# Last tile of a decoder kernel: where the output norm's power, the weights' splits and the norms of expert 0's base rows stand

## The reference

```python
x = x + attn(layernorm(x), ...)                  # blockwise attention
x = x + xattn(layernorm(x), ctx, ...)            # 16 heads, output normed with ln_scale, ln_bias
x = x + ffn(layernorm(x), Wr, br, W1, b1, W2, b2)

def ffn(inputs, Wr, br, W1, b1, W2, b2):         # N = 4096 rows, E = 8, C = 512
    probs = softmax(x @ Wr + br)
    gate, idx = max(probs), argmax(probs)
    pos = cumsum(one_hot(idx)) * one_hot(idx)    # place in the expert; kept where pos < C
    h = relu(expert_in @ W1 + b1)                # expert_in: rows gathered by (idx, pos), times gate
    eo = h @ W2 + b2
    out = gate * eo, put back to the rows
```

## Time and profile before

| what | us |
|---|---|
| median of 3 runs | 1316.72 |
| lowest and highest of them | 1315.18, 1317.61 |
| span of the profiled execution | 1317.2 |

### The profile page before, as it was taken

One profiled execution on the slowest core, in us unless ns is written; L12 is line 12 of the kernel. 1 busy time (PEld: TensorE's weight loads), 2 busy tenths in 40 slices (PEclk: granted clock), 3 DMA queues, 4 the chain that ended last, 5 costly groups with the idle time before them and its releaser, 6 DMA issues.

```text
span 1317.2 us, 31656 instructions
## 1 busy us (share of the span) xinstructions
PE 1286.3 (98%) x12357; PEld 1042.3 (79%) x12357; DVE 937.1 (71%) x1879; ACT 668.0 (51%) x1868; POOL 413.6 (31%) x477
## 2 busy tenths in 40 slices
PE   8999999999999999999999999999999999999998
PEld 7978667777777788888888888888888886888886
DVE  6539778888776676777767777777776786665563
ACT  4447434333333655655556555565555663654552
POOL 3213445454442012213131222312211223455453
PEclk9999999999999999999999999999999999999999
DMA  8962142232323201103021021120202103665530
GB/s 263 325 227 65 58 154 81 84 98 75 107 87 124 81 9 41 49 17 105 17 73 50 18 87 36 41 81 9 73 25 89 65 10 129 228 195 177 177 104 22
DMA packets 69233, 123.75 MB, mean 94 GB/s; under 512 B 12313, under 2 KB 20529, under 8 KB 69090
## 3 DMA queue, kind: packets, MB, share of 16 engines
q1 hardware_dynamic: 60770, 98.17, 22.4%
q0 software_dynamic: 8320, 23.62, 5.1%
HBM read 83.19 MB, written 42.07 MB: 95 GB/s over the span
## 4 chain that ended last, share of the span: by engine, by line
PE 80%; DVE 9%; ACT 4%; DMA 4%; issue 2%; SPq 1%; POOL 0%; DVEq 0%; POOLq 0%; ACTq 0%
PE bank L71 18%; PE bank L73 16%; PE bank L72 16%; PE bank L2335 6%; PE bank L2323 6%; PE bank L2356 4%; PE bank L2348 2%; PE bank L1269 2%; PE bank L1299 2%; DMA raw<-in_L_xattn_Wkv_dram 1%; ACT b_prob L1640 1%; PE bank L1243 1%; DMA raw<-in_L_attn_Wqkv_dram 1%; PE bank L2407 1%; PE bank L2888 1%
## 5 line engine op out<-in xcount | busy, mean ns | idle before, releaser
L1640 ACT ACTIVATE b_prob<-bank,b_neg_top 128x155 f32<-128x155 f32 x496 | 187.3, 407 | 115.6 <-DVE b_neg_top L1852 106.1
L71 PE MATMUL bank<-turned_h,big_h 128*128 128x512 f32 x320 | 130.8, 409 | 1.1 <-DVE turned_l L2106 0.8
L73 PE MATMUL bank<-turned_h,big_l 128*128 128x512 f32 x320 | 125.3, 392 | 0.0
L72 PE MATMUL bank<-turned_l,big_h 128*128 128x512 f32 x320 | 124.9, 390 | 0.0
L1852 DVE TENSOR_REDUCE b_neg_top<-bank 128x6 f32<-128x930 f32 (+1 forms) x93 | 94.4, 1015 | 31.4 <-PE bank L2335 30.3
L71 PE MATMUL bank<-b_wo_h,b_ot_h 128*128 128x512 f32 x256 | 113.1, 442 | 0.2 <-DVE b_ot_l L1881 0.2
L2323 PEld LDWEIGHTS bank<-ident,b_prob 128*128 128x128 f32 x640 | 93.5, 191 | 19.8 <-issue 5.7
L2323 PE MATMUL bank<-ident,b_prob 128*128 128x128 f32 x640 | 103.2, 284 | 1.8 <-DVE b_pt L1869 1.0
L1640 ACT ACTIVATION_READ_ACCUMULATOR b_prob<-bank,b_neg_top 128x1 f32 x496 | 102.7, 207 | 0.0
L73 PE MATMUL bank<-b_wo_h,b_ot_l 128*128 128x512 f32 x256 | 101.7, 397 | 0.0
L1863 DVE TENSOR_TENSOR b_prob<-b_prob,b_recip 128x930 f32<-128x930 f32 (+1 forms) x93 | 98.2, 1056 | 3.2
(11 more groups left out here) (358 smaller groups left out, 3347.9 us busy)
## 6 DMA issues: line engine op xcount, KB each, us to landing
wide<-in_L_ffn_W_dram SPq DMA_DIRECT2D x16, 1024.0 KB, 5.2
slot_rows<-empty_row SPq DMA_DIRECT2D x8, 1032.0 KB, 14.7
a_xr<-in_x_dram SPq DMA_DIRECT2D x32, 256.0 KB, 2.6
x_scratch<-a_xr SPq DMA_DIRECT2D x32, 256.0 KB, 2.1
tiles<-x_scratch SPq DMA_DIRECT2D x32, 256.0 KB, 3.7
rows<-x_scratch SPq DMA_DIRECT2D x32, 256.0 KB, 3.5
out_dram<-rows SPq DMA_DIRECT2D x32, 256.0 KB, 2.0
rows<-slot_rows SPq DMA_DIRECT2D x7, 1032.0 KB, 8.0
```

Of the source, the lines that this page charges most:

```text
L71: pe.matmul(out, lh, rh, start=first, stop=False)
L72: pe.matmul(out, lh, rl, start=False, stop=False)
L73: return pe.matmul(out, ll, rh, start=False, stop=last)
L1640: last = act.activation(prob[:, n % 2, j, h:h + 2 * L2 - 1:2], s_banks[:, h, o:o + L2], ACT.Exp, bias=neg_top[:, n % 2, h, j:j + 1], accum ...
```

## The change

Four edits, all in the last tile:

1. POOL, step `n == NT`: of the three scatters of batch `LAST - 1`, one stays ahead of `power("w", n)`, two come behind it.
2. DVE, step `n == NT`: `add_residual(n - 1)` and what follows it come ahead of `expert_split(4)` and `(5)`; these two take the place that `(6)` and `(7)` had; `(6)` moves behind `route_last`, `(7)` behind the four `first_rest`.
3. ACT, step `n == NT`: `first_norm(0)` and `(1)` move from ahead of `mine` to behind `mine_h`; `first_norm(2)` and `(3)` leave ACT.
4. DVE makes `first_norm(2)` and `(3)`, behind `route_last`, with one `tensor_scalar` each and a semaphore of their own, `first_normed2`; PE and SP wait for the new one where they need it.

PE's order and SP's order of transfers stay as they are.

```diff
@@ POOL
             if n == NT:
                 power("y", n - 1)
-                scatter(LAST - 1)
+                scatter(LAST - 1, 0, 1)
                 power("w", n)
+                scatter(LAST - 1, 1)
                 return
@@ ACT
                 route_exp(LAST)
-                first_norm(0)
-                first_norm(1)
                 need(act, s["route_step"], BASE[LAST] + 10)
...
                 act.activation(mine_h[:, :], mine[:, :], ACT.Copy).then_inc(s["mine_high"], 1)
-                first_norm(2)
-                first_norm(3)
+                first_norm(0)
+                first_norm(1)
@@ DVE
+        def first_norm(k):
+            dve.wait_ge(first_rows[k], 16)
+            dve.tensor_scalar(xn[:, k, :], rows[:, 0, k, 0:D], rows[:, 0, k, D + 3:D + 4], rows[:, 0, k, D + 2:D + 3],
+                              ALU.mult, ALU.add).then_inc(s["first_normed2"], 1)
...
                 w_stats(n - 1)
-                expert_split(4)
-                expert_split(5)
                 add_residual(n - 1)
                 need(dve, s["x2_made"], n)
                 norm_stats("y", n, row(n - 1), EPS1)
                 add_counts(LAST - 1)
-                expert_split(6)
-                expert_split(7)
+                expert_split(4)
+                expert_split(5)
                 logits(n - 1)
                 route_last()
+                first_norm(2)
+                first_norm(3)
+                expert_split(6)
                 for k in range(KD):
                     first_rest(k)
+                expert_split(7)
@@ PE, turn_first(k)
-            need(pe, s["first_normed"], k + 1)
+            if k < G // 2:
+                need(pe, s["first_normed"], k + 1)
+            else:
+                need(pe, s["first_normed2"], k - G // 2 + 1)
@@ SP, ahead of L2723
-            sp.wait_ge(late["first_normed"], G)
+            sp.wait_ge(late["first_normed"], G // 2)
+            sp.wait_ge(late["first_normed2"], G // 2)
```

More of the change, by code:

```diff
@@ L1473, in cross_attention @@
              "route_step route_exp counted counts_read routed scattered expert_high expert_low first_normed "
-             "first_turned first_high first_low numbered placed mine_normed mine_high mine_low").split()
+             "first_normed2 first_turned first_high first_low numbered placed mine_normed mine_high mine_low").split()
     s = {n: sem("b_" + n) for n in names}
@@ L2635, in cross_attention @@
     return dict(w_done=s["w_done"], outputs=NT, scattered=s["scattered"], sent=SENT[LAST + 1], first_rows=first_rows,
-                first_normed=s["first_normed"], first_low=s["first_low"], expert_low=s["expert_low"])
+                first_normed=s["first_normed"], first_normed2=s["first_normed2"], first_low=s["first_low"], expert_low=s["expert_low"])
 def experts(nc, block, sem, sb, late, bank, slot_tiles, out_rows, w1, b1, w2, b2, ident, big_h, big_l, y, xt_h,
```

## The result

| | before | after |
|---|---|---|
| median, us | 1316.53 (6 runs, 1315.18 to 1317.61) | 1321.57 (6 runs, 1319.93 to 1323.92) |
| ratio, 95% interval | | 1.0035 (1.0024 to 1.0047) |
| span of the profiled execution, us | 1317.2 | 1322.2 |
| its own time, us | not recorded | 1323.92 |

The change makes the kernel 5.0 us slower; the interval of the ratio is 3.2 to 6.2 us. I had forecast 1320.2, within 1317.3 to 1322.0. The execution profiled after is the slowest of its six. Of all the executions in this document one, of before_twin at 1402.65 us, was in a slow state, and it is left out of every time and ratio.

The account below looks back on a forecast made before the run. PE's own chain was taken to bind, through the start of expert 0's first product. Path +2.0 and clock +1.5 make +3.5 us on the median 1316.72: 1320.2 us, range 1317.3 to 1322.0.

Parts of the forecast that it names:

- What bounds the kernel: PE's own chain binds; the kernel's end moves with the start of expert 0's first product, at 1119.56.
- The chain through DRAM: Last row's scatter, load of expert 1's rows (6.82 us), ACT's relu at 1130.74; forecast to have slack.
- rival (c): The DRAM trip decides and the kernel isn't slower: 1316.0, with 0.25 and at most 0.47 us gained; chance 0.08.
- Edits 1 and 2: Residual some 2.5 us earlier, but warm multiplications leave PE's turn of the last tile only 0.25 us gain.
- That SP's load is late: Two scatters behind the power delay SP's first load of expert 0's rows about 0.6 us, free while covered.
- Edit 3: PE's first turn waits for ACT's norm of tile 0: 1115.21 in place of 1112.46, idle 2.9 us.
- path term: PE's fourth turn starts at 1119.66 against 1117.67: path 2.0 us longer, bounds 1.8 to 2.3.
- Edit 4: DVE's two norms end by 1116.5, ahead of PE's third turn at 1117.84; cost nothing, cover 1.3 us.
- The clock: PE's 2.9 us idle time brings a half-clock stretch over turns and picks: 1.5 us, floor 0, ceiling 3.3.
- rival (b): Two slow stretches or more, as PE doesn't get its clock back at once: 1322.0; chance 0.12.
- (a): The clock holds through the idle time and only the longer path counts: 1318.7; chance 0.25.
- (d): POOL's power is slow between scatters, the residual comes no earlier, 0.25 is lost: 1320.5; no chance of its own.

Follow-up runs that it names:

- before_twin: The kernel before, built once more with nothing changed; ratio 1.0007 (0.9992 to 1.0022).
- a_residual: The kernel before with only the residual's edits: POOL's power behind one scatter, DVE's residual ahead of all weight splits; ratio 0.9998.
- c_after_filled: The changed kernel plus three warm multiplications in PE's idle time ahead of its first turn; ratio 1.0023.
- d_norms_ahead: The changed kernel with ACT's norms of tiles 0 and 1 put back ahead of the last tile's own row; ratio 1.0013.
- after_third: The changed kernel timed and profiled a third time, nothing altered; ratio 1.0033 against before.
- after_again: The changed kernel timed and profiled a second time, nothing altered; ratio 1.0053 against before.
- b_norms_behind: The kernel before with only ACT's order changed: all four norms behind the last tile's own row, none on DVE; ratio 1.0038.
- the two filled kernels: The kernel before with only ACT's order changed, and the changed kernel, each with three warm multiplications in PE's idle time; ratios 1.0018 and 1.0023.

## Why the prediction was right, and where it was off

**What bounds the kernel** held. The chain through DRAM was rightly set aside: the product's place and the span moved together (5.03 and 5.0), and the chain of the changed kernel runs over ACT and PE. One price in rival (c) was misread: the 0.47 from 1132.41 to 1132.88 isn't PE's wait, since a multiplication of 0.39 starts at 1132.41, and only 0.08 of it is idle.

**Edits 1 and 2.** The gain of 0.25 on PE's turn was 0.26. The power took 0.88 us between the scatters, not 0.58, so the residual started at 1104.98 and not 1104.6; `warm` hid that. That SP's load is late was sized at 0.6 us and was 0.9 (1109.57 against 1108.55, counted from the warm multiplications). The statement that it costs nothing while ACT wants the rows later holds for the changed kernel; the cost when the cover is gone was named, 0.6 at most, and a_residual measures more: 0.47 late in place of 0.26 early, 0.73. The last tile's row on ACT came 0.34 earlier and not 0.25, because PE's turn, besides starting 0.26 earlier, took 0.60 in place of 0.66.

**Edit 3.** `turn_first(0)` was forecast at 1115.21 and stood at 1115.29; the idle time at 2.9 us and was 2.98. The path term of 2.0 is 2.14 by c_after_filled. The rest is the first two turns, which take 1.78 and not 1.62 from start to start. Two smaller errors cancel: the handover from ACT to PE was taken as 0.05 from DVE's row and was 0.14, and ACT's norm started 0.1 earlier than forecast, so that the first turn stands at +13.49 where the forecast had +13.50.

**Edit 4.** DVE's norms were done at 1116.58, ahead of the third turn, as forecast. d_norms_ahead loses that cover because DVE is 0.8 later there and PE 2 us earlier.

**The clock.** The mechanism was right, its size was the mis-sized term: 1.5 us forecast, 2.80 in the profile, 1.38 and 2.67 in the other two. The step that failed is the reason given against rival (b), that slow stretches had ended after one because they were filled with work. They had, but this one begins inside the idle time: PE is slow and idle for its first 0.9 us, and the clock came back only after 6.8 us. In after_third it was 1.2 and again 6.8 us, in after_again 0.5 and 3.4. That the idle share at its start is what made a stretch long fits these three and isn't shown. Rival (b) had 1322.0 and 0.12; it is what two of three profiles show, and the median lies 0.4 us inside the end of the range that this rival had set. That 1321.57 lies inside the range therefore owes something to luck: its upper end came from a rival that the text argued against. The text was also too sure of the fall itself: b_norms_behind kept its clock through 3.00 us. The median, 5.04 above before, is the path's 2.14 and 2.9 beside it. How much of those 2.9 is the clock of this stage in the median execution is not measured; the profiles give 1.4 to 2.8, the recorded clocks of all executions 1.5 to 2.8 lost at full clock, and the medians of the two filled kernels lie 0.7 and 0.5 above their paths with the clock full in the profile, which leaves 2.2 to 2.4.

**Rivals.** (a), the path alone, 1318.7, is what filling the idle time gives (1.0018 and 1.0023). (c) is out. (d), a power slowed between scatters, happened by 0.3 us and cost nothing while the warm multiplications covered it.

## What to carry to other kernels

An activation that an engine makes while it waits is free only there; moved behind the thing it waited for, it delays everyone whose queue begins with it, and the work in that queue besides: here the first pick came 2.47 us later in b_norms_behind, about the 0.80 of one norm and the 1.78 of the two turns that now stand in front of it. Before an operand's producer is moved, the consumer's own order has to be read: with the consumer's queue left as it was, all that stood behind the first operand waited too. And an idle time of 3 us on TensorE is to be priced twice, once for itself and once for the work behind it, which may run at half clock; a filler in the idle time took the second price away in both kernels that had one, and a filler that is too long ahead of a wait hides gains made there.

## What the runs showed of the hardware

TensorE's clock did not answer to an idle time alike in each execution: with 3 us of it, the clock fell in three of four profiles, 1.8 to 2.5 us after PE had stopped, and stayed low for 3.4 us in one and 6.8 us in the two others. The power on POOL between two scatters took 0.86 to 0.90 us in all kernels that had it there, against 0.58 behind three scatters. That the scatters are the reason isn't shown: the same instruction for the last tile's other statistics took 0.94 us before, after 2.2 us in which POOL did nothing, and 0.71 behind two scatters in the changed kernel.
